# Where the expert results are gathered: the first half's during the expert stage, the second half's one gather a step behind the score products

## The chip, the core and the metric

The kernel runs on one core of a Trainium2 chip. The metric is device time in microseconds from start to end of one execution, the median of several runs. The engines are TensorE (PE, with its weight loads PEld), VectorE (DVE), ScalarE (ACT), GpSimd (POOL) and the DMA queues; SyncE (SP) issues the plain transfers, GpSimd the indirect ones.

## The reference

64 samples of 128 tokens with 128 features go through two layers, every one with a residual connection and a tanh gate:

```python
x = x + tanh(g_xattn[0]) * L0_xattn(layernorm(x), ctx)    # 8 heads of 64, 77 keys
x = x + tanh(g_ffn[0])   * L0_ffn(layernorm(x))           # mixture of experts, best 2 of 16
x = x + tanh(g_xattn[1]) * L1_xattn(layernorm(x), ctx)    # 16 heads of 8, 77 keys
x = x + tanh(g_ffn[1])   * L1_ffn(layernorm(x))           # fp8-rounded 128 x 128 product

def L0_ffn(x):                                            # per token
    vals, idx = top_k(x @ Wg + bg + bias, 2)
    w = softmax(vals)
    y[e] = relu(x @ W1[e] + b1[e]) @ W2[e] + b2[e]
    return w[0] * y[idx[0]] + w[1] * y[idx[1]]
```

The third line reads, for each token, the two rows that its two experts have made. These reads are what is moved here.

## The kernel before, in words

The residual of all 64 samples stays in SBUF (`XR`). The work is done in three stages, and in each all engines run the same software pipeline: a loop over steps `t`, in which the part with lag `k` works on sample (or tile) `t - k`. Each engine waits for the others by semaphores that count samples.

**Stage A** is the first attention. It leaves the normalised expert input of sample b in `XN` (tile name `moe_in`, 64 blocks of 128 x 128). GpSimd scatters these rows, sorted by expert, into a DRAM buffer (`moe_rows`), two indirect DMAs a sample (line 521). The samples are two halves ("chunks") of 32, each with its own buffers `xs_flat[c]`, `ys_flat[c]`. The scatters of the second half run into stage B. After its scatter a block of `XN` is read by nobody.

**Stage B** (`step_b`) runs the experts on 160 tiles of 128 rows: tiles 0 to 79 are the first half, 80 to 159 the second. Groups of four tiles are loaded by SyncE (line 428, 256 KB) into one of two buffers, transposed (PE, line 1323), multiplied, biased (DVE, lines 1050 and 1057), rectified (ACT, line 722), and stored to `moe_results` (line 435). A loop body holds 32 tiles.

**Stage C** (`step_c`) is 81 steps, all written out without a loop. At step t:

- GpSimd issues `gather(b)` for sample b = t: two indirect DMAs (line 598), which bring the token's first and second expert row into `gy[0][p]` and `gy[1][p]`, a pair of buffers for each parity p of b. Before them it waits until x2 of sample b - 2 is made, since that frees the buffers. On GpSimd's queue they stand behind the bias addition of sample t - 3 (line 610), and in front of y4b (line 618, sample t - 15), the three fp8 rounding operations (lines 623, 625, 629, sample t - 12; the last makes `xq4`, which PE transposes in the next step at line 1352), and the power that makes the reciprocal root of the two variances (line 640).
- DVE adds the rows of sample t - 1 to the residual, with weights: `uc` (line 1078) and x2 (line 1100); then come statistics (lines 1127, 1136) and the variance (line 1156), for which GpSimd's line 640 waits, and for that DVE's normalisation of the next step (line 1088).
- PE has an order of its own: Q projection and transposes; S1, the scores of sample t - 5 (4 products), and ST, the transposed scores of sample t - 6; then, each at a wait for DVE's two row maxima (line 1070), the output product Y1, the key product KT and the transpose of the maxima; then V1, denominators and numerators. The first wait before S1 is for `OT1_made`: DVE's scaled numerators (line 1146) of the step before.
- ACT's step begins with a wait for `ST_mm`, the signal of the last ST product. Behind it stand two copies (line 659), the exponential (line 748), the copy of V1 and the Q bias (line 758), which PE's next step needs.
- DVE's line 1105 stands behind a wait for `KT_mm`, the signal of KT.

The arrays of one stage lie over those of another in one SBUF tile, `arena`. The buffers of stage C's gathers (`gy`) lie behind the end of stage B's arrays. In stage B GpSimd can therefore issue gathers already, but only those of samples 0 and 1, since sample 2 needs x2 of sample 0. It waits first until the results of the chunk are stored (`ys_stored`).

## Time and profile before

| What | us |
|---|---|
| median of 3 runs | 1195.06 |
| lowest and highest | 1191.57, 1212.96 |
| the profiled execution | 1195.27 |
| its span in the profile | 1193.4 |
| stage B in the span | about 480 to 724 |
| stage C in the span | about 724 to 1193 |

The profile covers one execution, 1.87 us shorter than that execution's own time, since start and end of the program lie outside it. "Busy" of an engine is the time in which it executed something, not time in which it did useful work at full rate. The ends of PE's instructions are modelled by the profile, their starts are recorded. A figure in brackets behind an instruction is the time that its engine stood idle before it and what ended that idle time; "issue" stands where no releaser is shown.

### The profile page before, as it was taken

The numbers are of one execution on the slowest core, as the hardware profiler recorded it, in microseconds if no ns is written. First come the engines' busy times: TensorE is split into PE (matmuls) and PEld (weight loads), VectorE is DVE, ScalarE is ACT, GpSimd is POOL, SyncE is SP. The second block draws the span as 40 slices with busy tenths as digits, with TensorE's granted clock in tenths as the row PEclk, the third lists the DMA queues.
The fourth block names the chain that finished last, engine by engine and source line by source line (L and its number), as shares of the span: only waits on it lengthen the run. The fifth ranks groups of instructions, "written<-read, shape, count | busy, mean of one in ns | idle before, by whom it ended". The sixth has DMA issues, their size and how long they took to land. (4 is left out here: it accounts for less than half of the span.)

```text
span 1193.4 us, 41254 instructions
## 1 busy us (share of the span) xinstructions
PE 1052.4 (88%) x13498; PEld 848.3 (71%) x13499; DVE 822.2 (69%) x2573; ACT 588.0 (49%) x1415; POOL 648.9 (54%) x1155
## 2 busy tenths in 40 slices
PE   4999999979999993898899996899999999998893
PEld 4788787856877772677777784677777777776672
DVE  1777777786777776444444445678888888887784
ACT  2666666644656651334344441335555454544454
POOL 2333333324777776666620004467777777777755
PEclk9999999998999997899999997999999999999997
DMA  3321122222334201244343332111111111111101
GB/s 73 86 50 43 38 52 69 68 66 70 98 90 104 70 23 39 86 125 122 111 112 88 88 88 58 32 29 36 43 41 45 40 45 39 45 41 40 41 23 31
DMA packets 106888, 74.21 MB, mean 62 GB/s; under 512 B 21360, under 2 KB 98288, under 8 KB 106736
## 3 DMA queue, kind: packets, MB, share of 16 engines
q1 hardware_dynamic: 98544, 55.40, 17.9%
q0 software_dynamic: 8192, 16.79, 4.7%
q8 instruction: 93, 1.52, 0.6%
q14 instruction: 59, 0.48, 0.1%
HBM read 38.60 MB, written 33.55 MB: 60 GB/s over the span
## 5 line engine op out<-in xcount | busy, mean ns | idle before, releaser
L659 ACT ACTIVATE arena<-PS 77x512 f32<-77x512 f32 (+4 forms) x736 | 305.1, 441 | 464.5 <-PE PS L1177 270.7
L1177 PE MATMUL PS<-arena 128*32 128x128 f32 (+5 forms) x9488 | 452.9, 291 | 50.2 <-issue 16.6
L1177 PEld LDWEIGHTS PS<-arena 128*32 128x32 f32 (+4 forms) x9488 | 352.4, 145 | 129.4 <-issue 36.5
L1177 PE MATMUL PS<-w,arena 128*128 x960 | 199.8, 325 | 9.0 <-issue 7.1
L521 POOL DMA_INDIRECT moe_rows<-arena x128 | 127.4, 996 | 71.7 <-POOL arena L517 50.3
L1177 PEld LDWEIGHTS PS<-w,arena 128*128 128x128 f32 x960 | 135.5, 195 | 29.8 <-issue 17.8
L640 POOL TENSOR_TENSOR arena<-arena,minus_half 128x2 f32<-128x2 f32 (+1 forms) x71 | 51.2, 721 | 189.4 <-DVE arena L1156 185.5
L598 POOL DMA_INDIRECT arena<-moe_results,slot x128 | 128.7, 1005 | 43.8 <-issue 31.6
L536 POOL TENSOR_TENSOR arena<-arena,minus_half 128x2 f32<-128x2 f32 (+1 forms) x70 | 47.6, 680 | 187.9 <-DVE arena L834 166.4
L1057 DVE TENSOR_TENSOR arena<-PS,b_rows 128x256 f32<-128x256 f32 x160 | 67.8, 424 | 90.0 <-PE PS L1177 74.4
L1177 PEld LDWEIGHTS PS<-arena,wk_wq 128*128 128x128 f32 x512 | 80.4, 198 | 45.5 <-issue 43.0
L722 ACT ACTIVATE arena<-PS 128x256 f32<-128x256 f32 x160 | 61.3, 383 | 82.6 <-PE PS L1309 76.0
L1177 PE MATMUL PS<-wo,arena 128*128 128x128 f32 x640 | 99.7, 287 | 2.0 <-ACT arena L659 1.1
L1177 PE MATMUL PS<-arena,wk_wq 128*128 128x154 f32 x512 | 98.1, 316 | 1.5 <-ACT arena L659 0.8
L1070 DVE TENSOR_REDUCE arena<-PS 128x8 f32<-128x616 f32 x128 | 96.0, 792 | 2.8 <-PE PS L1177 2.8
L748 ACT ACTIVATE arena<-PS 128x1536 f32<-128x1536 f32 x64 | 93.3, 1458 | 0.0
L1177 PEld LDWEIGHTS PS<-wo,arena 128*128 128x128 f32 x640 | 83.7, 193 | 13.1 <-ACT arena L659 2.9
L543 POOL TENSOR_TENSOR arena<-arena 128x616 f32<-128x616 f32 x64 | 78.1, 1220 | 21.9 <-DVE arena L900 21.8
L871 DVE TENSOR_REDUCE arena<-PS 128x8 f32<-128x616 f32 x64 | 51.2, 800 | 54.4 <-PE PS L1177 53.1
L1050 DVE TENSOR_TENSOR arena<-PS,b_rows 128x128 f32<-128x128 f32 x160 | 46.3, 289 | 41.7 <-PE PS L1177 33.7
L1254 PE MATMUL PS<-ident,arena 128*77 128x128 f32 x512 | 68.8, 277 | 1.3 <-ACT arena L659 1.3
L1131 DVE RECIPROCAL arena<-PS 128x128 f32<-128x128 f32 x64 | 61.1, 955 | 12.5 <-PE PS L1177 8.6
(151 smaller groups left out, 1657.9 us busy)
## 6 DMA issues: line engine op xcount, KB each, us to landing
moe_rows<-zeros SPq DMA_DIRECT2D x64, 160.0 KB, 2.5
arena<-moe_rows SPq DMA_DIRECT2D x40, 256.0 KB
moe_results<-arena SPq DMA_DIRECT2D x40, 256.0 KB
residual<-in_x SPq DMA_DIRECT2D x64, 64.0 KB
w<-in_W SPq DMA_DIRECT2D x32, 128.0 KB
arena<-in_ctxC SPq DMA_DIRECT2D x64, 64.0 KB
out<-arena SPq DMA_DIRECT2D x64, 64.0 KB, 1.6
arena<-in_ctxT SPq DMA_DIRECT2D x32, 77.0 KB
```

The lines of the kernel that those rows point to most:

```text
L521: g.indirect_dma_start(out=xs_flat[c][:, :], out_offset=bass.IndirectOffsetOnAxis(ap=si[2 * p + k], axis=0), in_=scat[p], in_offset=None). ...
L543: g.tensor_tensor(pv, pv, rd0[t.par(3)].rearrange("q (h o) -> q h o", o=1).to_broadcast([P, H0, J]), ALU.mult).then_inc(s["P0_made"], 1)
L598: g.indirect_dma_start(out=gy[k][p], out_offset=None, in_=ys_flat[c][:, :], in_offset=bass.IndirectOffsetOnAxis(ap=POS[k][:, b:b + 1], axi ...
L640: g.tensor_tensor(rsc[t.par(0)][:, cols], vc[t.par(0)][:, cols], mhalf[:, cols], ALU.pow).then_inc(s["rsc_made"], 1)
L659: A.activation(o, i, ACT.Copy).then_inc(s[done], 1)
L722: A.activation(hT[p], PS[:, 4 + p, 0:EH], ACT.Relu).then_inc(s["hT_cp"], 1)
L748: A.activation(PT1[t.par(6)].rearrange("q (g w) -> q g w", g=NG), PS[:, 4:4 + NG, 0:TAIL], ACT.Exp, scale=DH1 ** -0.5).then_inc(s["exp1"], 1)
L1057: V.tensor_tensor(hb[p], PS[:, 2 + p, 0:EH], b1s[:, bass.ds(e, 1), :].rearrange("q o h -> q (o h)"), ALU.add).then_inc(s["h_made"], 1)
L1070: V.tensor_reduce(mx1[:, 2 * i * KEYS:2 * (i + 1) * KEYS].rearrange("q (g k) -> q g k", g=2)[:, :, 0:GH], PS[:, 2 * i:2 * i + 2, 0:GH * J] ...
L1131: V.reciprocal(rd1, PS[:, 1, 0:P]).then_inc(s["rd1_made"], 1)
L1177: return T.matmul(o, l, r, start=start, stop=stop)
L1254: last = T.transpose(PS[0:J, 2 + h // HB0, (h % HB0) * P:(h % HB0 + 1) * P], P0[p][:, h * J:(h + 1) * J], ident[:, :])
```

## The change

- `gy` is gone. A gather now writes into `XN`: row k of sample b goes to block `k * 32 + b % 32`. So sample b and b + 32 share a place, and no sample within one half does.
- GpSimd issues all 64 gathers of the first half in front of stage C's first step, as soon as the first half's results are stored, that is, during stage B.
- In stage C GpSimd issues only the second half's 64 gathers: two a step in steps 4 to 9, one a step in steps 10 to 61. The wait for the second half's stored results moves from step 32 to step 4. The wait for x2 is now for sample b - 32, and there is one for the completion of all gathers of the same parity before it.
- Their place on GpSimd's queue is behind y4b, in front of the fp8 rounding, and each step's gather waits for `ST_mm`, the signal for which ACT waits too.
- DVE's lines 1078 and 1100 read `XN` in place of `gy`. Nothing else is changed, but that every line behind the edit has a higher number (598 becomes 605, 610 becomes 629, 618 becomes 635, 623, 625, 629 become 645, 647, 651, and 640 becomes 662).

```diff
--- before.py
+++ after.py
@@ -244,8 +244,7 @@
 
         PT1 = [cc(NG * TAIL) for _ in range(2)]
         KB1 = [cc(GH * KW) for _ in range(2)]
-        assert cc.at >= cb.at
-        gy = [[cc(D) for _ in range(2)] for _ in range(2)]
+        cc.at = max(cc.at, cb.at)
         ctxc = [cc(KW + KEYS) for _ in range(4)]
         one_hot = cc(GH * KW)
         sum1 = cc(NKB * KEYS)
@@ -314,6 +313,11 @@
 
             engine.nop(nofuse=True)
 
+        def gathered(b, k):
+
+            at = k * CB + b % CB
+            return XN[:, at:at + 1, :].rearrange("q o d -> q (o d)")
+
         def row(ap, parts=P):
 
             return ap.rearrange("(o n) -> o n", o=1).to_broadcast([parts, ap.shape[0]])
@@ -591,12 +595,27 @@
                               wv1[:, :].rearrange("q (g e) -> q g e", g=NG)[:, :, q * DH1:(q + 1) * DH1]).then_inc(s["c_consts"], 1)
             pool.wait_ge(s["c_consts"], 4 + 5 * GH)
 
-            def gather(b, p, c):
-                wait_free(pool, s["x2_made"], b - 1)
+            def gather(b, k):
+
+                p = b % 2
+                if k == 0:
+                    wait_free(pool, s[f"gy_made{p}"], (b - p) * 16)
+                    wait_free(pool, s["x2_made"], b - CB + 1)
                 apart(pool)
+                g.indirect_dma_start(out=gathered(b, k), out_offset=None, in_=ys_flat[b // CB][:, :],
+                                     in_offset=bass.IndirectOffsetOnAxis(ap=POS[k][:, b:b + 1], axis=0)).then_inc(s[f"gy_made{p}"], 16)
+
+            for p in range(2):
+                pool.wait_ge(s[f"ys_stored{p}"], NG_B // 2 * 16)
+            for b in range(CB):
                 for k in range(2):
-                    g.indirect_dma_start(out=gy[k][p], out_offset=None, in_=ys_flat[c][:, :],
-                                         in_offset=bass.IndirectOffsetOnAxis(ap=POS[k][:, b:b + 1], axis=0)).then_inc(s[f"gy_made{p}"], 16)
+                    gather(b, k)
+
+            def gathers_of(t):
+
+                one_at, two_at = 10, 4
+                j = 2 * (t - two_at) if t < one_at else 2 * (one_at - two_at) + t - one_at
+                return [(CB + i // 2, i % 2) for i in range(j, j + (2 if t < one_at else 1)) if 0 <= i < 2 * CB]
 
             def step_c(t):
                 if (b := t.at(12)) is not None:
@@ -609,13 +628,16 @@
                     pool.wait_ge(s["xn3_made"], b + 1)
                     g.tensor_tensor(XR[:, bass.ds(b, 1), :].rearrange("q o d -> q (o d)"),
                                     XR[:, bass.ds(b, 1), :].rearrange("q o d -> q (o d)"), bo1[:, :], ALU.add).then_inc(s["x2b_made"], 1)
-                if (b := t.at(0)) is not None:
-                    gather(b, t.par(0), t.chunk)
                 if (b := t.at(15)) is not None:
                     p = t.par(15)
                     pool.wait_ge(s["y4_made"], b + 1)
                     wait_free(pool, s["obs_made"], b - 1)
                     g.tensor_tensor(y4b[p], y4[p], fbias[:, :], ALU.add).then_inc(s["y4b_made"], 1)
+                if gathers_of(t.value):
+
+                    wait_free(pool, s["ST_mm"], t.seen(6, 1))
+                for b, k in gathers_of(t.value):
+                    gather(b, k)
                 if (b := t.at(12)) is not None:
                     p = t.par(12)
 
@@ -640,13 +662,11 @@
                     g.tensor_tensor(rsc[t.par(0)][:, cols], vc[t.par(0)][:, cols], mhalf[:, cols], ALU.pow).then_inc(s["rsc_made"], 1)
 
             for first, last, peeled in c_spans():
-                if first in (0, CB):
-
-                    for p in range(2):
-                        pool.wait_ge(s[f"ys_stored{p}"], (NCH if first else 1) * NG_B // 2 * 16)
 
                 def step(t):
-                    t.chunk = 0 if first < CB else 1
+                    if t.value == 4:
+                        for p in range(2):
+                            pool.wait_ge(s[f"ys_stored{p}"], NCH * NG_B // 2 * 16)
                     step_c(t)
                 run_steps(pool, NB, first, last, peeled, step, TURN, LEADC)
 
@@ -1075,7 +1095,7 @@
                     p = t.par(1)
                     dve.wait_ge(s[f"gy_made{p}"], (b - p) * 16 + 32)
                     wait_free(dve, s["x2_made"], b)
-                    V.scalar_tensor_tensor(uc, gy[0][p], WT[0][:, bass.ds(b, 1)], res(b), ALU.mult, ALU.add).then_inc(s["u_made"], 1)
+                    V.scalar_tensor_tensor(uc, gathered(b, 0), WT[0][:, bass.ds(b, 1)], res(b), ALU.mult, ALU.add).then_inc(s["u_made"], 1)
                 if (b := t.at(11)) is not None:
                     p = t.par(11)
                     dve.wait_ge(s["z4_made"], b + 1)
@@ -1097,7 +1117,7 @@
                 if (b := t.at(1)) is not None:
                     p = t.par(1)
                     dve.wait_ge(s["u_made"], b + 1)
-                    V.scalar_tensor_tensor(res(b), gy[1][p], WT[1][:, bass.ds(b, 1)], uc, ALU.mult, ALU.add).then_inc(s["x2_made"], 1)
+                    V.scalar_tensor_tensor(res(b), gathered(b, 1), WT[1][:, bass.ds(b, 1)], uc, ALU.mult, ALU.add).then_inc(s["x2_made"], 1)
                 wait_free(dve, s["KT_mm"], t.seen(4, 1))
                 if (b := t.at(8)) is not None:
                     wait_edge(dve, t, s["Y1_mm"], b + 1)
```

GpSimd's instructions from the last set-up copy to the start of stage C. `moe_results` is the expert results in DRAM, `moe_in` is `XN`, `slot` the row numbers. Before:

```order
L590 COPY arena<-wv 128x4x8
L598 DMA arena<-moe_results,slot 128x128 x4
L640 TENSOR_TENSOR arena<-arena,minus_half 128x1
L598 DMA arena<-moe_results,slot 128x128 x2
L640 TENSOR_TENSOR arena<-arena,minus_half 128x1
L610 TENSOR_TENSOR residual<-residual,bo 128x128
L598 DMA arena<-moe_results,slot 128x128 x2
```

After:

```order
L594 COPY arena<-wv 128x4x8
L605 DMA moe_in<-moe_results,slot 128x128 x64
L662 TENSOR_TENSOR arena<-arena,minus_half 128x1 x2
L629 TENSOR_TENSOR residual<-residual,bo 128x128
L662 TENSOR_TENSOR arena<-arena,minus_half 128x1
L629 TENSOR_TENSOR residual<-residual,bo 128x128
L605 DMA moe_in<-moe_results,slot 128x128 x2
```

The first row of gathers has 64 where it had four, the ones of steps 2 and 3 are gone, and from step 4 on there are two a step, as before.

GpSimd's queue in one full step of stage C. Before, with the bias addition, the gathers, y4b, the three rounding operations and the power:

```order
L606 TENSOR_SCALAR arena<-arena 128x128
L610 TENSOR_TENSOR residual<-residual,bo 128x128
L598 DMA arena<-moe_results,slot 128x128 x2
L618 TENSOR_TENSOR arena<-arena,ffn_bias 128x128
L623 TENSOR_TENSOR arena<-arena 128x128
L625 TENSOR_TENSOR arena<-arena 128x128
L629 TENSOR_TENSOR arena<-arena 128x128
L640 TENSOR_TENSOR arena<-arena,minus_half 128x2
```

After:

```order
L625 TENSOR_SCALAR arena<-arena 128x128
L629 TENSOR_TENSOR residual<-residual,bo 128x128
L635 TENSOR_TENSOR arena<-arena,ffn_bias 128x128
L605 DMA moe_in<-moe_results,slot 128x128
L645 TENSOR_TENSOR arena<-arena 128x128
L647 TENSOR_TENSOR arena<-arena 128x128
L651 TENSOR_TENSOR arena<-arena 128x128
L662 TENSOR_TENSOR arena<-arena,minus_half 128x2
```

One of the two gathers has gone, and the other stands behind the addition of `ffn_bias` (y4b) instead of in front of it.

## Rows read from the trace of the kernel before

**Rows 1.** The page: span, and busy time of two engines.

```profile
span 1193.4 us, 41254 instructions
PE 1052.4 (88%) x13498; PEld 848.3 (71%) x13499; DVE 822.2 (69%) x2573; ACT 588.0 (49%) x1415; POOL 648.9 (54%) x1155
```

**Rows 2.** Stretches: length, busy PE PEld DVE ACT POOL, clock, DMA share, GB/s.

```profile
507.00:588.00 81.00, 71.74 (x459) 59.57 (x458) 34.02 (x100) 31.46 (x100) 55.17 (x113) 0.96 0.40 121
641.00:709.00 68.00, 63.80 (x434) 53.65 (x433) 32.97 (x96) 31.70 (x96) 0.00 (x0) 1.00 0.32 93
850.00:1070.00 220.00, 204.09 (x4552) 165.96 (x4549) 187.55 (x592) 112.34 (x296) 172.64 (x296) 1.00 0.15 42
```

**Rows 3.** Line 1146, one a step, in 850:1078 and in 1085:1135.

```profile
L1146 DVE TENSOR_TENSOR arena<-PS,arena x35: 292/292/293, 849.9 to 1077.4; 128x128 f32<-128x128 f32 x35
L1146 DVE TENSOR_TENSOR arena<-PS,arena x6: 292/292/292, 1091.8 to 1128.3; 128x128 f32<-128x128 f32 x6
```

**Rows 4.** Timeline of step 30 (start, duration, what, idle before).

```profile
903.75 2.14 PE L1177 MATMUL PS<-arena 32*128 32x308 f32 x56 [0.15 <-DVE arena L1146]
...
905.57 1.06 POOL L598 DMA_INDIRECT arena<-moe_results,slot  x1 [0.17 <-issue]
...
906.87 0.45 ACT L659 ACTIVATE arena<-PS 128x128 bf16<-128x128 bf16 x2 [3.27 <-PE PS L1177]
906.94 0.95 POOL L598 DMA_INDIRECT arena<-moe_results,slot  x1 [0.30 <-issue]
...
907.60 0.35 DVE L1105 SCALAR_TENSOR_TENSOR residual<-PS,tanh_gates,residual 128x128 f32<-128x128 f32 x1 [0.60 <-PE PS L1177]
...
908.30 0.46 POOL L623 TENSOR_TENSOR arena<-arena 128x128 f32<-128x128 f32 x1
908.30 1.34 PE L1177 MATMUL PS<-arena 128*32 128x128 f32 x40 [0.31 <-issue]
...
909.43 0.45 POOL L629 TENSOR_TENSOR arena<-arena 128x128 bf16<-128x128 f32 x1
```

**Rows 5.** Timeline of step 64, the first without gathers.

```profile
1136.35 2.14 PE L1177 MATMUL PS<-arena 32*128 32x308 f32 x56
...
1138.55 0.45 ACT L659 ACTIVATE arena<-PS 128x128 bf16<-128x128 bf16 x2 [1.90 <-PE PS L1177]
...
1140.72 0.96 DVE L1131 RECIPROCAL arena<-PS 128x128 f32<-128x128 f32 x1 [0.30 <-PE PS L1177]
...
1142.12 2.14 PE L1177 MATMUL PS<-arena 32*128 32x308 f32 x56 [0.17 <-DVE arena L1146]
```

**Rows 6.** Timelines: a late scatter, a late gather, and step 58 after it.

```profile
568.90 0.97 POOL L521 DMA_INDIRECT moe_rows<-arena  x1 [2.22 <-issue]
...
1081.96 0.95 POOL L598 DMA_INDIRECT arena<-moe_results,slot  x1 [1.37 <-issue]
...
1092.56 2.14 PE L1177 MATMUL PS<-arena 32*128 32x308 f32 x56
...
1096.71 0.45 ACT L659 ACTIVATE arena<-PS 128x128 bf16<-128x128 bf16 x2 [3.84 <-remote]
```

**Rows 7.** Stage B: tiles and scatters in the two stretches; stores during four gathers.

```profile
L1323 PEld LDWEIGHTS PS<-ident,arena x50: 137/141/230, 507.9 to 586.9; 128*128 128x128 f32 x50
L521 POOL DMA_INDIRECT moe_rows<-arena x45: 954/966/982, 506.5 to 586.7; - x45
...
L1323 PEld LDWEIGHTS PS<-ident,arena x48: 137/141/143, 641.4 to 708.2; 128*128 128x128 f32 x48
...
615.79 0.38 SPq L435 DMA_DIRECT2D moe_results<-arena  x1
...
622.77 0.38 SPq L435 DMA_DIRECT2D moe_results<-arena  x1
```

**Rows 8.** Line 598 in the whole span, and who waited for it.

```profile
L598 POOL DMA_INDIRECT arena<-moe_results,slot x128: 940/978/1082, 614.2 to 1131.8; - x128
...
  DVE arena L1078: 5.5, 3
```

## The prediction

> **What bounds the kernel now.** I read the page first. PE is busy for 88% of the span, DVE for 69%, GpSimd for 54% [rows 1]. The shares by stage say more: in stage C PE is busy for 204.09 of 220 us and DVE for 187.55, GpSimd for 172.64, at full granted clock and with the DMA engines at 0.15 [rows 2]. So no transfer bounds stage C, and PE and DVE are both near full. The chain of waits ends in the last samples' short steps and tells nothing of the steady state, so I went to one line that runs once a step. Line 1146 starts 35 times between 849.9 and 1077.4, which is 6.69 us a step. Later it starts 6 times between 1091.8 and 1128.3, which is 7.30 us [rows 3]. The same work runs in two rhythms.
>
> The timeline of one step shows what makes them. All offsets are from the start of the score products (S1 and ST, 56 instructions), which the profile lets end after 2.14 us. With gathers, ACT's first instruction, released by `ST_mm`, comes at 906.87 - 903.75 = +3.12, and DVE's line 1105, released by `KT_mm`, at +3.85; the two gathers start at +1.82 and +3.19 [rows 4]. In step 64, which has all of PE's work but no gather, ACT starts at 1138.55 - 1136.35 = +2.20, and the next step begins after 5.77 us [rows 5]. In the slow rhythm ACT starts at 1096.71 - 1092.56 = +4.15 [rows 6]. The signal of a finished product thus reaches its waiter 0.9 to 1.9 us late when a gather is being issued. And PE pauses within its products (0.31 us, no releaser) at 908.30, 1.36 us after the second gather's start [rows 4]; step 64 has no such pause. I take this for an effect of the gather instruction, and the forecast rests on it. It matters because PE's next step waits for ACT (Q bias) and for DVE (line 1146), whose work starts with these signals.
>
> The slow rhythm begins behind one late gather, at 1081.96 with 1.37 us of idle time in front. A scatter was late too, by 2.22 us at 568.90 [rows 6]. Counted over all indirect DMAs these are numbers 114 and 242, 128 apart, so I expect number 242 to be late again.
>
> **What the change costs in stage B.** 64 gathers run there in place of 4. One takes 0.978 us [rows 8] and 0.30 us of idle time stands before it [rows 4]: 64 x 1.28 = 82 us, from 614.2 to about 696. Stage B ends at 724, so GpSimd is done in time. Nothing waits on GpSimd's queue then, and DVE reads the rows after 724. The cost is what PE, ACT and DVE lose, and two rows price it:
>
> - Beside scatters, 50 tiles start in 507.9 to 586.9, 79.0 / 49 = 1.61 us a tile; without indirect DMAs 48 in 641.4 to 708.2, 66.8 / 47 = 1.42 [rows 7]. That is 0.19 x 50 = 9.5 us for 45 scatters, 0.21 us each. The first stretch has two loop turns and the second one, so a part of it is not the scatters'.
> - The four gathers of today: the store of one group is issued at 615.79 and of the next at 622.77 [rows 7]. A group is four tiles, 4 x 1.42 = 5.68 us, so 6.98 - 5.68 = 1.30 us were lost to the three gathers within it, 0.43 each.
>
> The gathers are denser than the scatters and write no DRAM. I take 0.25, near the row with 45 cases: 64 x 0.25 = +16 us. The ends are half the scatter's price, 0.11 (+7; PE waits for its loads in this stage and can lose some time unnoticed), and the burst's 0.43 (+28).
>
> **The start of stage C.** Today DVE's line 1078 waits 5.5 us in three cases for gathers just issued [rows 8]. Afterwards the rows are there, and steps 2 and 3 lose both gathers from GpSimd's queue, in front of the power for which DVE waits. From step 4 on GpSimd has two again. DVE's own chain then takes over a part: -3 us (ends -1 and -5).
>
> **The steady steps.** From step 10 on one gather is issued, about 0.15 us behind `ST_mm`. ACT is then released at +2.2. The gather starts at +2.35 and ends at +3.35, and the three rounding operations follow; they took 1.58 us from 908.30 to 909.88 [rows 4], so `xq4` is there at +5.0, where it now comes at 909.88 - 903.75 = +6.13. What is late next is `KT_mm`. If a gather holds signals until 1.30 us after its start, as the first one does now (905.57 to 906.87), DVE's line 1105 starts at +3.65 in place of +3.85. Its chain from there to the next score products is now 903.75 + 6.69 - 907.60 = 2.84 us, which gives 6.5. But a part of this chain is a wait for PE's later products, which a single gather delays less. Without a gather the step took 1142.12 - 1136.35 = 5.77 [rows 5]; PE's pause of 0.31, put on top, gives 6.1. I take 6.3, the middle of the two. The lower end is 6.0: DVE's own load is 187.55 / 220 x 6.69 = 5.70 [rows 2], and it has waits besides. The upper end is 6.6: less than the 0.2 at `KT_mm` is won.
>
> - Steps 10 to 55: 46 x (6.69 - 6.3) = -17.9.
> - Steps 56 to 61, now in the slow rhythm: 6 x (7.30 - 6.3) = -6.0.
> - Steps 62 and 63, which lose their last gathers: 2 x (7.30 - 6.2) = -2.2.
> - The late indirect DMA: after 128 scatters, 64 + 12 gathers, number 242 is the 38th single one, in step 47. It delays `xq4` by 1.37, from +5.0 to about the start of PE's next step: +1.
>
> Steps 4 to 9 keep two gathers, now behind `ST_mm`: I count nothing. The wait moved to step 4 is for the stores of stage B, which all engines pass anyway. The waits for sample b - 32 and for earlier gathers are over long before. Sum: 16 - 3 - 17.9 - 6.0 - 2.2 + 1 = -12.1. The profiled execution took 1195.27 (median 1195.06, so it stands for the runs): **1183**.
>
> With the ends for B and C: 7 - 3 - 46 x 0.69 - 6 x 1.30 - 2.2 + 1 = -37 gives 1158; 28 - 3 - 46 x 0.09 - 6 x 0.70 - 2.2 + 1 = +15 gives 1211.
>
> **A rule that speaks against it.** The trace shows PE and ACT late beside GpSimd's gathers [rows 4, 5]. The Trainium skill, "SBUF — State Buffer", section "Who interferes with whom", says that only DVE and GpSimd share a port, that "PE and ACT never wait on anyone", and that a DMA never contends with a compute engine. By that rule the moved gather frees only GpSimd's queue, which is rival A. The trace contradicts it as far as one step without gathers can; that step's lighter DVE queue in the next one is the doubt.
>
> **Rivals.**
>
> A. The signals are late for another reason, and the steady period stays 6.69. For it: in the fast rhythm PE also waits 0.15 us for line 1146, so DVE may simply be the bound. Against it: ACT's +3.12 and +2.20 with equal PE work. Then B's price stays, and the late gather moves from step 56 to step 47 and starts the slow rhythm earlier: 14 steps at +0.61 in place of 6. Time: 1195.27 + 16 - 3 + 8 x 0.61 = 1213, and with the burst's price 1225. This is the slower case; it decides from the point where the steady steps win less than 13 us together. Chance 0.15.
>
> B. The signals of KT come in time behind a single gather too, DVE's load is all that is left, and the gathers in stage B hide in PE's waits for loads. For it: DVE waits only 0.60 us for KT now, with two gathers. Time 1158. Chance 0.22.
>
> C. Stage B pays the burst's price throughout, since 64 gathers stand back to back as those four did, and stage C wins as forecast: 1195.27 + 28 - 3 - 26.1 + 1 = 1195. Chance 0.15.
>
> The forecast has 0.48. Within 2% of the median is 1171.2 to 1219.0, about what a measurement tells from no change. Faster: B and the forecast's lower edge, 0.28. Slower: half of A, 0.07. Same: 0.65. The range 1158 to 1211 takes in C and B's value and leaves the far part of A out.
>
> **What would show the steps right or wrong.** ACT's first instruction at +2.2 and the gather right behind it; line 1146 every 6.3 us from step 10 on, no 7.3; 1.6 to 1.7 us a tile from 614 to 696; DVE's line 1078 never waiting for a gather; one gather near step 47 with over 1 us of idle time in front. If ACT starts at +3 although no gather is under way, my reading of the signals is wrong. If tiles in stage B take 2 us, its price is.

## The result and the profile after

The changed kernel takes 1237.04 us (median of four runs, 1229.77 to 1243.78) against 1193.42 us for the kernel before in the same series. The ratio is 1.037, 95% interval 1.029 to 1.045: slower, where the prediction had 1183 and "same" as the likeliest outcome. In three of the six series of runs (this first one and two of the experiments) the kernel before took 1193 to 1202 us, in the other three 1153 to 1154. I call them series of the first and of the second kind; the section "Two kinds of series" shows what differs between them in the traces, though not what sets it.

The stretches of the changed kernel (length, busy PE PEld DVE ACT POOL with the number of instructions, granted clock, DMA share, GB/s): beside the scatters, beside the moved gathers, behind them, and in the steady part of stage C.

```profile
507.00:588.00 81.00, 69.17 (x440) 57.30 (x439) 32.73 (x97) 30.59 (x98) 53.98 (x111) 0.96 0.40 118
616.00:696.00 80.00, 19.10 (x88) 12.88 (x87) 6.18 (x18) 5.15 (x17) 59.58 (x64) 0.59 0.22 64
707.00:775.00 68.00, 63.50 (x416) 53.55 (x417) 32.95 (x96) 30.86 (x96) 0.00 (x0) 0.96 0.32 93
890.00:1070.00 180.00, 177.00 (x4082) 146.09 (x4084) 166.32 (x535) 104.26 (x266) 130.78 (x237) 1.00 0.12 35
```

The first and third row look like their counterparts of before [rows 2]. The second is the result: for 80 us PE does almost nothing, 19.10 us of work, and with it DVE and ACT. GpSimd has its 64 gathers and nothing else, and the DMA engines are at 0.22, so no transfer fills the time. The granted clock of 0.59 is not the cause, since the pauses come first. The clock falls to 0.5, the lower of its two levels, at 630.4 us, but already between 621 and 630, at 1.00, PE is busy for only 4.78 of 9 us:

```profile
621.00:630.00 9.00, 4.78 (x27) 3.46 (x28) 1.96 (x6) 1.82 (x7) 6.01 (x8) 1.00 0.28 83
```

The fourth row answers to the stage C of before: PE is busy for 177.00 of 180 us in place of 204.09 of 220.

The next view is the timeline inside that hole (start, duration, engine, line, what, and in brackets the idle time before it with its inferred releaser).

```profile
633.73 0.69 PE L1329 MATMUL PS<-ident,arena 128*128 128x128 f32 x2 [2.88 <-DVE arena L1077]
...
652.85 0.42 DVE L1077 TENSOR_TENSOR arena<-PS,b_rows 128x256 f32<-128x256 f32 x1 [10.17 <-remote]
653.33 0.69 PE L1329 MATMUL PS<-ident,arena 128*128 128x128 f32 x2 [4.25 <-issue]
653.51 0.94 POOL L605 DMA_INDIRECT moe_in<-moe_results,slot  x1 [0.30 <-DMA moe_in<-moe_results,slot]
654.76 0.95 POOL L605 DMA_INDIRECT moe_in<-moe_results,slot  x1 [0.31 <-issue]
...
672.25 0.38 ACT L742 ACTIVATE arena<-PS 128x256 f32<-128x256 f32 x1 [16.52 <-issue]
673.08 0.93 PEld L1197 LDWEIGHTS PS<-w,arena 128*128 128x128 f32 x4 [16.21 <-issue]
...
696.75 0.38 ACT L742 ACTIVATE arena<-PS 128x256 f32<-128x256 f32 x1 [15.13 <-remote]
```

Read it in both directions. DVE's line 1077 makes `h` and ends at 653.27; PE's transposes of `h` (line 1329) start at 653.33. So a signal of DVE reaches PE in 0.06 us, and ACT's end at 672.63 is answered by PE within 0.5.

The other direction needs care. Transposes and copies of them by ACT (line 742, which needs nothing but `hT_mm`) can't be paired by looking for the next copy, since PE may run two tiles ahead: each product has two buffers in PSUM. They can be paired by number. The trace holds every one of them in this stage, two transposes and one copy for each of the 160 tiles. Paired so, with times from the trace:

```
tile               85      86      89      90      91      92      93      94      95
transposes end  617.64  618.85  624.62  626.32  634.42  654.02  679.28  703.78  709.26
copy starts     617.67  620.67  629.49  647.05  672.25  696.75  706.66  707.10  709.30
late by           0.04    1.82    4.87   20.73   37.83   42.74   27.38    3.32    0.04
```

So the copy at 672.25 belongs to the transposes that started at 633.73, and those of 653.33 are taken up at 696.75, 42.7 us late. The other three signals that PE gives for each tile are as late: `xsT_mm` by up to 47.0 us, `h_mm` by 45.3, `y_mm` by 42.3. In the middle of the hole they are answered in the order in which PE produced them, one about every 5.4 us (eight of them from 666.76 to 704.45), which is one for four gathers. At 657.5 eight handovers are open, two for each of the four signals, and that is as far as the two buffers let PE run ahead. Only what comes out of PE is late. The releaser names ("issue", "remote") are no help there; but where the trace has the event of the semaphore itself, it lies just before ACT's start (`hT_mm` at 696.73), so it isn't ACT that is slow to react. The gathers go on every 1.25 us through all of it. Nor does the loading of instructions differ: its queue moves one packet in 618 to 668, as in `b_no_gather` below.

The hole doesn't open with the first gather, and it doesn't close with the last. The same view at its two edges:

```profile
616.35 1.01 POOL L605 DMA_INDIRECT moe_in<-moe_results,slot  x1 [15.53 <-DMA moe_results<-arena]
616.47 0.38 ACT L742 ACTIVATE arena<-PS 128x256 f32<-128x256 f32 x1 [0.39 <-PE PS L1329]
...
618.46 0.38 PE L1329 MATMUL PS<-ident,arena 128*128 128x128 f32 x2
...
620.67 0.38 ACT L742 ACTIVATE arena<-PS 128x256 f32<-128x256 f32 x1 [1.98 <-PE PS L1329]
...
695.95 0.94 POOL L605 DMA_INDIRECT moe_in<-moe_results,slot  x1 [0.30 <-issue]
...
703.09 0.69 PE L1329 MATMUL PS<-ident,arena 128*128 128x128 f32 x2 [4.51 <-DVE arena L1077]
...
707.10 0.39 ACT L742 ACTIVATE arena<-PS 128x256 f32<-128x256 f32 x1
```

The transposes that end at 616.43, with the first gather under way, are taken up 0.04 us later; those that end at 618.84 (tile 86) are taken up 1.83 us later. And the transposes that end at 703.78, almost 7 us after the last gather, still reach ACT 3.3 us late, although in 700 to 707 the trace has no packet of any DMA queue. Then seven open handovers are answered between 706.66 and 707.63, and from 709.30 on a copy starts 0.04 us behind its transposes again. So it is a backlog: the signals of PE's ends queue up, are let through one by one while gathers are issued, and need 10 us after the last gather to drain.

Stage C, one step (start, duration, what, idle before):

```profile
963.80 1.18 PE L1197 MATMUL PS<-arena 32*128 32x128 f32 x36
...
965.06 0.45 ACT L679 ACTIVATE arena<-PS 128x128 bf16<-128x128 bf16 x2 [2.10 <-PE PS L1197]
...
965.81 1.25 POOL L605 DMA_INDIRECT moe_in<-moe_results,slot  x1 [0.94 <-PE PS L1197]
966.01 0.34 DVE L1125 SCALAR_TENSOR_TENSOR residual<-PS,tanh_gates,residual 128x128 f32<-128x128 f32 x1
...
967.48 0.96 DVE L1151 RECIPROCAL arena<-PS 128x128 f32<-128x128 f32 x1 [0.20 <-PE PS L1197]
...
968.21 0.46 POOL L651 TENSOR_TENSOR arena<-arena 128x128 bf16<-128x128 f32 x1
...
968.89 2.14 PE L1197 MATMUL PS<-arena 32*128 32x308 f32 x56
```

The step's score products started at 962.85, one period of 6.04 before those at 968.89. ACT is released at +2.21, where it was at +3.12 [rows 4]; the gather starts at +2.96, where the prediction had +2.35; line 1125 no longer waits for PE; the rounding chain ends at +5.8, where the prediction had +5.0. DVE has two gaps in the step, 0.22 and 0.20. The period is 6.04, in place of 6.69 and 7.30 [rows 3].

The late indirect DMAs, from the same view: one scatter, one gather. They are numbers 114 and 242 again [rows 6].

```profile
566.90 0.96 POOL L525 DMA_INDIRECT moe_rows<-arena  x1 [2.22 <-issue]
...
1078.27 1.09 POOL L605 DMA_INDIRECT moe_in<-moe_results,slot  x1 [3.66 <-issue]
```

The balance of the two profiled executions, from the starts of lines in their traces (the last expert result is the last of line 1070, 801.3 with its duration):

```
part                                         before    after     difference
up to tile 80 of the experts                  610.8    612.9       +2.1
second half of the experts (80 tiles)         113.4    188.4      +75.0
from there to the score products of step 5     11.1      8.3       -2.8
steps 5 to 9                                   33.8     37.5       +3.7
steps 10 to 55                                308.5    283.9      -24.6
steps 56 to 61                                 44.0     36.3       -7.8
steps 62 and 63                                14.6     12.1       -2.5
rest, and around the span                      59.0     59.2       +0.2
sum                                          1195.3   1238.6      +43.3
```

### The profile page after: what moved, and what is told of

It reads as the page before. It is cut to its first block and busy times, and to the rows that moved or that the text cites. A ratio compares the mean times of both kernels' runs of the same rounds, so it can differ in the third digit from the quotient of the medians.

```text
span 1236.7 us, 41310 instructions
## 1 busy us (share of the span) xinstructions
PE 1051.2 (85%) x13498; PEld 850.0 (69%) x13499; DVE 819.9 (66%) x2573; ACT 594.1 (48%) x1415; POOL 654.3 (53%) x1155
## 5 line engine op out<-in xcount | busy, mean ns | idle before, releaser
L1197 PE MATMUL PS<-arena 128*32 128x128 f32 (+5 forms) x9488 | 436.9, 292 | 31.8 <-DMA logit_bias<-in_bias 12.4
L1197 PE MATMUL PS<-w,arena 128*128 x960 | 206.8, 333 | 58.4 <-issue 54.6
L1197 PEld LDWEIGHTS PS<-w,arena 128*128 128x128 f32 x960 | 140.2, 201 | 81.7 <-issue 70.4
L605 POOL DMA_INDIRECT moe_in<-moe_results,slot x128 | 133.6, 1043 | 106.5 <-PE PS L1197 61.8
L1329 PE MATMUL PS<-ident,arena 128*128 128x128 f32 x320 | 64.8, 286 | 18.5 <-DVE arena L1077 13.0
```

The costliest lines, as they stand in the source:

```text
L605: g.indirect_dma_start(out=gathered(b, k), out_offset=None, in_=ys_flat[b // CB][:, :], in_offset=bass.IndirectOffsetOnAxis(ap=POS[k][:, b ...
L1197: return T.matmul(o, l, r, start=start, stop=stop)
L1329: last = T.transpose(PS[:, 4 + p, q * P:(q + 1) * P], hb[p][:, q * P:(q + 1) * P], ident[:, :])
```

## Experiments

Theory T: indirect gathers issued by GpSimd delay the ends of PE's work on their way to the engines that wait for them; with pauses between gathers they pass, back to back they starve. The rivals for the expert stage: the traffic, any work of GpSimd, a fixed price wherever a gather lies. For stage C: is it the place of the gather or their number that gives the gain?

### What in the moved gathers costs the time (first kind of series, before at 1201.17)

`b_no_gather`: the loop is gone, so the first half's expert results are left out, and the counts in the waits are lowered accordingly.

```diff
-            for b in range(CB):
-                for k in range(2):
-                    gather(b, k)
```

> The changed kernel without the 64 gathers beside the second half of the expert stage (left out of the computation: the expert results of the first half's blocks; the last stage reads what lies in their rows). Theory T, the stall is made by the gathers alone: the 77 us of the expert stage go, the rest stays: 1160 us, last expert result of the stage at 724. Rival, something else in the changed kernel (the waits for the stores, the new buffers) holds TensorE's signals: above 1200, the pauses of 14 to 25 us between tiles stay.

Measured: 1157.05, ratio 0.962 (0.959 to 0.965). The second half of the experts takes 111.3 us, against 188.4. All 55 copies of line 742 (738 here) in 616 to 696 start 0.04 us behind their transposes.

`b_busy_pool`: that kernel with other work for GpSimd.

```diff
...
+            for n in range(2):
...
+                for j in range(CB):
+                    two = XN[:, 2 * j:2 * j + 2, :].rearrange("q o d -> q (o d)")
+                    g.tensor_tensor(two, two, two, ALU.add).then_inc(s["c_consts"], 1)
```

> No gathers in the expert stage but 64 additions of 128x256 f32 in place on GpSimd, back to back, some 0.9 us each, in their rows (the first half's blocks lose their expert results). Theory T: GpSimd's own arithmetic holds nobody's signals: 1160 to 1170, no pause over 5 us between tiles. Rival B (any busy GpSimd does it, by the shared port or otherwise): near 1237, pauses of 14 to 25 us as before.

Measured: 1156.20, ratio 0.962 (0.960 to 0.965); 112.2 us for the half. The additions took 0.57 us each in place of the 0.9 I wanted, so GpSimd was busy without a pause for 36 us and not for 80. No copy in this time is late.

`b_plain_dma`: the same bytes, without indices.

```diff
...
-                    gather(b, k)
+                    apart(pool)
+                    g.dma_start(gathered(b, k), ys_flat[0][(2 * b + k) * P:(2 * b + k + 1) * P, :]).then_inc(s[f"gy_made{p}"], 16)
```

> The 64 indirect gathers of the expert stage replaced by 64 plain transfers of the same 64 KB each, issued by GpSimd too, into the same rows (what it changes in the computation: the first half's blocks get rows in order instead of by index). Theory T (GpSimd's work of an indirect gather holds the signals): 1160 to 1170. Rival D (the traffic of the DMA engines or of HBM does it, whoever asks for it): 1237 again, last expert result at 801.

Measured: 1166.66, ratio 0.972 (0.968 to 0.975); 117.2 us for the half. Here too no copy is late: the price of these transfers isn't in the signals.

`b_one_a_tile`: all 64 gathers, paced.

```diff
             for b in range(CB):
                 for k in range(2):
+                    pool.wait_ge(s["y_made"], NT + 4 + 2 * b + k)
                     gather(b, k)
```

> The same 64 gathers, but each waits until one more tile of the expert stage is done, so one a tile of some 1.4 us instead of one per 1.25 us. Theory T (back-to-back gathers starve TensorE's signals, a pause lets them through): the long pauses go, some 0.3 us a gather stays: 1160 + 19 = about 1180, between 1170 and 1195. Rival P (each gather has a fixed price of 1.2 us wherever it lies in this stage): 1237, with the loss spread over 64 tiles in place of a few long pauses.

Measured: 1178.99, ratio 0.982 (0.978 to 0.986); 134.3 us for the half. Nothing is left out of the computation, and the ratio to the kernel before lies below 1. Of the 66 copies in 613 to 728, 28 are late, by at most 2.46 us.

The same stretch, 616 to 696, in the four kernels, in the order above (columns as before):

```profile
616.00:696.00 80.00, 74.15 (x503) 62.05 (x501) 38.08 (x111) 36.61 (x112) 0.00 (x0) 1.00 0.31 91
```

```profile
616.00:696.00 80.00, 74.23 (x495) 62.42 (x493) 37.85 (x111) 36.25 (x110) 31.87 (x56) 0.98 0.31 88
```

```profile
616.00:696.00 80.00, 68.70 (x463) 57.18 (x461) 35.32 (x104) 34.06 (x103) 33.31 (x62) 1.00 0.49 138
```

```profile
616.00:696.00 80.00, 67.35 (x414) 54.13 (x413) 30.27 (x92) 27.23 (x92) 42.71 (x46) 0.96 0.41 112
```

PE's busy time tells it: 74 us with an idle or an adding GpSimd, 69 with plain transfers at a DMA share of 0.49, which is far more than the 0.22 of the changed kernel, and 19 with the dense gathers. So the stall is neither the traffic nor, as far as 36 us of additions show, GpSimd's being busy. Per gather, over the 111.3: (112.2 - 111.3) / 64 = 0.01 us for an addition, 0.09 for a plain transfer, 0.36 for a gather per tile, 1.20 for a dense one. The timeline of a paced stretch shows the mechanism at work:

```profile
654.41 0.95 POOL L605 DMA_INDIRECT moe_in<-moe_results,slot  x1 [2.35 <-DVE arena L1071]
...
655.78 0.95 POOL L605 DMA_INDIRECT moe_in<-moe_results,slot  x1 [0.42 <-DVE arena L1071]
...
656.31 0.38 PE L1330 MATMUL PS<-ident,arena 128*128 128x128 f32 x2
...
656.73 0.38 ACT L743 ACTIVATE arena<-PS 128x256 f32<-128x256 f32 x1 [0.39 <-issue]
...
657.03 0.95 POOL L605 DMA_INDIRECT moe_in<-moe_results,slot  x1 [0.30 <-issue]
...
657.52 0.38 PE L1330 MATMUL PS<-ident,arena 128*128 128x128 f32 x2
...
658.28 0.95 POOL L605 DMA_INDIRECT moe_in<-moe_results,slot  x1 [0.30 <-issue]
...
658.87 0.38 PE L1330 MATMUL PS<-ident,arena 128*128 128x128 f32 x2
...
660.28 0.39 ACT L743 ACTIVATE arena<-PS 128x256 f32<-128x256 f32 x1 [1.97 <-PE PS L1330]
...
661.50 0.95 POOL L605 DMA_INDIRECT moe_in<-moe_results,slot  x1 [2.27 <-DVE arena L1071]
```

Four gathers stand close together, as in the dense loop. The transposes that end at 656.69 are taken up after 0.04 us; those that end at 657.90 wait until 660.28. Then no tile has finished, so GpSimd waits 2.27 us with the next gather, and all catch up. That is the feedback that the dense loop lacks; the pattern comes back every 7.1 us, four tiles, where four tiles take 111.3 / 20 = 5.6 without gathers.

### Place or number in stage C

`c_two_placed`: the changed kernel with 6 gathers beside the experts and the rest two a step behind the score products.

```diff
-            for b in range(CB):
+            for b in range(3):
...
-                one_at, two_at = 10, 4
-                j = 2 * (t - two_at) if t < one_at else 2 * (one_at - two_at) + t - one_at
-                return [(CB + i // 2, i % 2) for i in range(j, j + (2 if t < one_at else 1)) if 0 <= i < 2 * CB]
+                return [(t + 3, k) for k in range(2) if t + 3 < NB]
...
-                    if t.value == 4:
+                    if t.value == CB - 3:
```

> The placement without the moving of half of the gathers: only 6 gathers stand in the expert stage, the rest two a step in the last stage, both behind the wait for the score products as in the changed kernel, three blocks ahead. Theory C (in the last stage it is the count that matters: a second gather behind the score products costs 1.3 us, as steps 8 and 9 of the changed kernel show with 7.4): period 7.4, so slower than the kernel before in this stage (6.7): about 1157 + 52 x 1.3 = 1225, between 1210 and 1245. Rival L (the place alone gives the gain; once no signal is waited for, a second gather is free): period 6.04 to 6.2, 1160 to 1170.

Measured (second kind, before at 1152.72): 1217.94, ratio 1.057 (1.054 to 1.060), 7.34 us in an ordinary step. The number is theory C's, the reason isn't. The timeline of GpSimd in step 30, whose score products start at 901.84:

```profile
904.82 1.06 POOL L605 DMA_INDIRECT moe_in<-moe_results,slot  x1 [1.41 <-PE PS L1195]
...
906.19 0.95 POOL L605 DMA_INDIRECT moe_in<-moe_results,slot  x1 [0.30 <-issue]
...
908.44 0.51 POOL L649 TENSOR_TENSOR arena<-arena 128x128 bf16<-128x128 f32 x1
...
909.01 0.23 PE L1370 MATMUL PS<-identb,arena 128*128 128x128 bf16 x1 [1.62 <-POOL arena L649]
```

ACT is released at +2.21 in the ordinary steps, so that signal isn't held; GpSimd's own queue is the bound. It waits 1.41 us for the score products, and its rounding (line 649) comes behind both gathers, with PE waiting 1.62 us for it, 83 us in all. In steps 8 to 11, before the rounding begins, the same two gathers leave steps of 5.97 to 6.22 us. Two gathers and the rounding behind that wait don't fit in a step. The run doesn't separate place and number.

`c_one_unplaced` does: the kernel before, its old place, one gather.

```diff
-                for k in range(2):
+                for k in range(1, 2):
                     g.indirect_dma_start(out=gy[k][p], out_offset=None, in_=ys_flat[c][:, :],
...
```

> The kernel before with one gather a step in place of two, at its old place ahead of the score products (the second expert's row is used twice and the first one's left out, in the computation). Theory C (the count decides): period close to 6.04 to 6.2, 1193 - 64 x 0.6 = about 1155, between 1145 and 1165. Rival L (the place decides: one gather ahead of the products still holds the signal that ScalarE waits for): period 6.4 to 6.7, 1175 to 1193.

Measured (second kind, 1152.72): 1144.04, ratio 0.991 (0.988 to 0.995), 6.03 us a step. The same again, in a series of the first kind (before at 1202.22):

> c_one_unplaced again. On a chip where the kernel before takes about 1153: 1144 as measured, 6.03 a step. On one where it takes about 1195: theory C (the count decides) 6.04 to 6.2 a step, 1150 to 1160; rival L (the place decides, one gather ahead of the products still holds the signal for ScalarE to +3.12) 6.4 to 6.7 a step, 1175 to 1193.

Measured: 1150.75, ratio 0.957 (0.953 to 0.961), 6.08 us a step (median of steps 18 to 45). One step each, first kind, then second:

```profile
848.78 2.14 PE L1177 MATMUL PS<-arena 32*128 32x308 f32 x56
850.33 1.07 POOL L598 DMA_INDIRECT arena<-moe_results,slot  x1 [0.17 <-issue]
851.74 0.45 ACT L659 ACTIVATE arena<-PS 128x128 bf16<-128x128 bf16 x2 [2.65 <-PE PS L1177]
...
854.86 0.54 PE L1177 MATMUL PS<-arena 32*128 32x308 f32 x4
```

```profile
846.34 2.14 PE L1177 MATMUL PS<-arena 32*128 32x308 f32 x56 [0.18 <-DVE arena L1146]
848.15 1.09 POOL L598 DMA_INDIRECT arena<-moe_results,slot  x1 [0.17 <-issue]
848.54 0.45 ACT L659 ACTIVATE arena<-PS 128x128 bf16<-128x128 bf16 x2 [2.52 <-PE PS L1177]
```

In the first, ACT starts at +2.96, 0.75 us late (0.91 with the two gathers of before), and still the step takes 6.08. So in stage C and in the first kind the number decides: one late signal per step is absorbed, and what costs 0.6 us (6.69 less 6.08) is the second gather. Rival L is right about the signal and wrong about its price. The placing behind `ST_mm`, which the change is built on, is worth next to nothing: steps 10 to 55 take 280.5 us here and 283.9 in the changed kernel, or 279.8 without the 4.1 us of its late gather, which this run with fewer gathers doesn't reach.

In the second kind the second gather at the old place costs little too: the whole kernel before is 8.7 us slower than this one (1152.72 against 1144.04), 0.14 us a step. There the place matters as soon as there are two: behind `ST_mm` two gathers make the step 7.34 us long, as `c_two_placed` shows.

The second timeline (second kind) shows something else. A gather is under way from 848.15, ACT needs a product that ended at 848.48, and starts at 848.54. This signal isn't held.

### Two kinds of series

> The changed kernel unedited, on whatever chip this job gets. The kernel before took 1193 to 1201 us in the first two jobs and 1153 in the third. Theory X (how much a gather holds TensorE's signals differs between chips): where the kernel before takes about 1153, the changed one has no starved expert stage and takes 1145 to 1155; where it takes about 1195, the changed one takes about 1237. Rival Y (only the kernel before has a second pace): 1237 beside either.

> The kernel before unedited, for its trace. Theory X: where it takes about 1153, its last stage runs at 6.04 us a step with ScalarE's first instruction at +2.21, with the same two gathers at +1.8 and +3.2; where it takes about 1195, 6.69 and +3.12 as in the first trace.

Both unedited, first kind (1202.22): the changed kernel 1236.44, ratio 1.028 (1.024 to 1.032), with the same hole in its trace (PE busy 19.11 us in 616 to 696); the kernel before 1207.38 in a single run, 6.77 us a step. And the last series, of the second kind (1153.68):

> The changed kernel unedited once more. Where the kernel before takes about 1153, theory X (there a gather holds no signal of TensorE): no starved expert stage, 1143 to 1152; rival Y (the back-to-back gathers starve the stage in any job): above 1200. Where it takes about 1200: 1237 as twice before.

Measured: 1151.25, ratio 0.998 (0.997 to 0.999). The same kernel, 85 us faster, and there is no hole. The stretch and the timeline beside its gathers:

```profile
605.00:691.00 86.00, 73.01 (x493) 60.92 (x492) 37.62 (x110) 36.06 (x110) 59.95 (x64) 1.00 0.48 128
```

```profile
640.10 0.38 PE L1329 MATMUL PS<-ident,arena 128*128 128x128 f32 x2
...
640.23 0.95 POOL L605 DMA_INDIRECT moe_in<-moe_results,slot  x1 [0.30 <-issue]
...
640.52 0.38 ACT L742 ACTIVATE arena<-PS 128x256 f32<-128x256 f32 x1 [0.39 <-PE PS L1329]
...
641.48 0.94 POOL L605 DMA_INDIRECT moe_in<-moe_results,slot  x1 [0.30 <-issue]
```

The gathers are as dense (median 1.249 us apart, as in the first profile) and as long. The transposes end at 640.48, with a gather under way, and ACT starts 0.04 us later, as do all 55 copies in this stretch. The second half of the experts takes 119.3 us against 112.5 in `c_one_unplaced`: 0.11 us a gather, about the price of a plain transfer. So theory X of `after_again2` holds: in the second kind a gather holds none of these signals. That it is the chip, as `after_again` had it, doesn't hold: chip 3 gave one series of each kind. What sets it stays open; no run here varied it, and there is no trace of the kernel before in the second kind.

### Pace and place of the gathers beside the experts

`b_pair_two_tiles` waits once per two tiles (`y_made` at NT + 4 + 2 b) and issues two gathers. Second kind, then first:

> As b_one_a_tile, but two gathers one behind the other every second tile, so 2.2 us held and then a pause. Theory T (held signals pass in the pause, and the engines then catch up): the same or a little more than one a tile, 1175 to 1195. Rival Q (a second gather right behind the first already starves the signals as in the changed kernel): above 1210.

> b_pair_two_tiles again. On a chip where the kernel before takes about 1153: 1147 as measured. On one where it takes about 1195: theory T 1175 to 1195, rival Q (a second gather right behind the first already starves the signals) above 1210.

Measured: 1147.43, ratio 0.996 (0.994 to 0.997); in the first kind 1185.52, ratio 0.986 (0.981 to 0.991), 137.0 us for the half, 0.40 us a gather. Rival Q falls: two in a row don't starve the stage when the next pair waits for tiles.

`b_spacer` has a fixed pause, two clearings with a wait on GpSimd behind each gather:

```diff
                     gather(b, k)
+                    pool.wait_ge(s["c_consts"], 4 + 5 * GH + 4 * b + 2 * k)
+                    g.memset(n4, 0.0).then_inc(s["c_consts"], 1)
+                    g.memset(t4, 0.0).then_inc(s["c_consts"], 1)
+            pool.wait_ge(s["c_consts"], 4 + 5 * GH + 4 * CB)
```

> The 64 gathers of the expert stage with a fixed pause in place of a wait for the tiles: behind each, two clearings of 128x128 on GpSimd, some 0.45 us, with a wait, so a gather per 1.6 to 1.7 us. Theory T (a pause lets the held signals through): no starving, 64 x 0.35 = 22 above 1157: 1175 to 1190. Rival K (it is the feedback that helps; a fixed pause lets a backlog build up): 1200 to 1240, pauses of over 10 us between tiles.

Measured: 1148.16, ratio 0.995, before at 1153.48, and 1149.49, ratio 0.997, in the last series. Both were of the second kind, so whether a fixed pause is enough stays open. So do two more, each seen only in the second kind: the place within a tile (`b_tile_xsT`, which waits for `xsT_mm` at NT + 9 + 2 b + k: 1150.08, ratio 0.997, and again 1150.12, 0.996) and five gathers to six tiles (`b_five_in_six`: 1144.89, ratio 0.992, 0.990 to 0.994).

> As b_one_a_tile, but each gather waits for TensorE's transpose of an input tile (its last work of a tile) in place of the tile's result on VectorE: the same number, another place within the tile. Theory T: the price is what signals a gather of 0.95 us holds; with four a tile of 1.4 us any place hits some: 1170 to 1190, as b_one_a_tile (1179 of 1201 before) within 8. Rival F (a place exists where nothing is waited for, as behind the score products of the last stage): 1160 to 1168.

> As b_one_a_tile, but five gathers to six tiles, over nearly the whole second half of the stage. Theory T (each gather holds a signal or two for up to 1 us, at a price each): the number is the same, so within 4 us of b_one_again, 1175 to 1183 where the kernel before takes about 1200. Rival N (the price falls with density): 5 to 10 us less.

`b_one_again` is the paced version once more:

> b_one_a_tile again, with more rounds, as the version that beat both kernels: where the kernel before takes about 1200, 1179 again, a ratio of 0.98; where it takes about 1153, 1148 and a ratio of 0.996.

Measured: 1146.31, ratio 0.9935 (0.992 to 0.995), before at 1153.48. One gather a tile thus beats the kernel before in both kinds, by 1.8% and by 0.65%, small but outside the intervals, and the changed kernel, compared by their ratios in different series, by about 5% (0.982 against 1.037 and 1.028) and by 0.5% (0.9935 against 0.998).

## Why the prediction was wrong

The range ended at 1211, the result is 1237. By its steps:

- **Stage B, the step that failed.** "The gathers are denser than the scatters and write no DRAM. I take 0.25, near the row with 45 cases", with the burst's 0.43 as the upper end. Measured: 1.20 us a gather, (188.4 - 111.3) / 64; +75 in place of +16. With that one term put right the sum would give 1242, and 1238.6 was measured. Neither row could give it. The 45 scatters are dense by number, but each pair stands behind three copies and so behind a pause; and the four gathers are a short burst in an otherwise free stage, which was over before a signal was more than 2.9 us late. The same four cost (113.4 - 111.3) / 4 = 0.5 each, so 0.43 was near the price of a burst of four. The sum multiplies a price of single gathers by 64, as if gathers were independent of each other, but the signals form a queue: behind the first gathers they are 2 us late, after eight 21, after thirty 43. What failed is the overlap: I took PE, ACT and DVE to go on beside the gathers with a small loss each, and they were stopped instead until the gathers were through. A sign stood in rows that I had: ACT late by 0.9 us in the fast rhythm and by 1.9 in the slow one with the same two gathers. In the slow one the signal didn't pass in the 0.30 us between them but only behind the second; so a second gather close behind the first can hold the same signal again. I used this for stage C and not for stage B.
- **Start of stage C:** -3 forecast, -2.8 measured.
- **Steps 4 to 9:** nothing counted, +3.7 measured in steps 5 to 9. Steps 6 and 7 took 8.4 and 9.2 us, and two gathers behind `ST_mm` make steps 8 and 9 7.4 us long; in a series of the second kind these four take 6.5, 6.0, 6.0 and 6.1.
- **Steps 10 to 55:** -17.9 + 1, with a period of 6.3; measured -24.6 with 6.04, the lower end (6.0). ACT comes at +2.21 as forecast, but that isn't what shortens the step: `c_one_again` has ACT at +2.96 and almost the same period, 6.08. The step is won by the gather that is gone, which the prediction had only in its remark that a single gather delays PE's later products less. Of the two estimates whose middle I took, 6.1 from the step without gathers was the better one.
- **Steps 56 to 63:** -8.2 forecast, -10.3 measured.
- **The late gather** came at step 47 as forecast, number 242, but 3.66 us late instead of 1.37: step 47 and the next took 8.70 and 7.46, +4.1 in place of +1.
- **The rivals.** A (period stays 6.69) fell, though its doubt whether ACT's late start sets the period was justified, and so did the hidden gathers of B, though B's stage C came true. C had the right stage and the right sign but the price of four gathers.
- **The page's rule.** In series of the first kind PE's results are late by up to 47 us while gathers are issued (49 in `after_again`), and in those of the second kind ACT takes them up within 0.04 us. The Trainium skill, "SBUF — State Buffer", section "Who interferes with whom", says that "PE and ACT never wait on anyone"; it speaks there of engines that contend for ports of SBUF. The prediction read it as a rule on signals too, and so read it would give the time of the second kind, which the first kind's traces contradict. Whether a port of SBUF has any part in the delay no run here shows.

What is shown: in series of the first kind, the stall needs the indirect gathers, isn't made by their traffic or by GpSimd's work as such, and shrinks to at most 3.3 us a signal with one gather a tile. What is only argued: that it is the signal which is late. For it speaks that PE starts work on the following tiles while up to eight of its signals are open. But the ends of PE's instructions are modelled in the profile, so the completion of PE's work itself might be what is late; the runs don't tell these apart. And why a gather holds it up, and only in series of the first kind, stays open.

## What to carry to other kernels

Price an operation that disturbs its neighbours at the density at which it will run: a price from spaced cases says nothing of a queue with no pause in it, and an engine that "has time" for 64 gathers may still have no time between them. When such work is moved beside a stage with many short handovers, pace it by that stage's own progress semaphore, which costs one wait and lets the stage slow it down. And compare versions within one series of runs, again in another: here the ratio of the same two kernels was 1.04 and 1.03 in two series and 1.00 in a third. When you read such a trace and the producer has several buffers, pair its work with its consumer's by number and not by the nearest time; otherwise a wait of 43 us looks like one of 18.

## What the hardware showed that I had not expected

- In series of the first kind, back-to-back indirect gathers (0.94 us each, 1.25 apart) cut PE's work beside them from 74 to 19 us in 80, through late ends of PE's work alone, up to 47 us late and answered in their order, one for about four gathers; DVE to PE took 0.06 us meanwhile. The delay needs a few gathers to build up and lasted 10 us beyond the last. With one gather a tile the price was 0.36 us, with plain transfers of the same bytes from the same engine 0.09.
- In series of the second kind, one of them on a chip that also gave the first, the same gathers cost 0.11 us and held none of the signals read here; the kernel before ran 4% faster (1153 against 1201).
- The indirect DMA number 242 was late in both kinds, by 3.66 us in the changed kernel and 1.37 in the kernel before, and number 114 by 2.22 in most traces (2.7 to 3.5 in four of them). In `b_plain_dma`, which has 64 plain transfers between them, the late one with 3.66 us was indirect DMA number 178, so 242 again if all that GpSimd issues is counted.
